# A chunked selective scan block on one core: the first step's sum kept in PSUM, its clip read from there, and first transposes a tile later

## The reference

```python
xr, gate = jnp.split(x @ W_in.T, 2, axis=-1)
xr = xr + t_emb[:, None, :]
xc = silu(depthwise_causal_conv4(xr, W_conv) + b_conv)
xn = (xc - mean(xc)) / jnp.sqrt(var(xc) + 1e-05) * ln_g + ln_b
Bm, Cm, dt = jnp.split(xn @ W_xproj.T, 3, axis=-1)
dt = jnp.tanh(dt @ W_dt.T + b_dt) * 0.01
Ad = 1.0 + dt * (-jnp.tanh(A_log))
Bd = Bm * jnp.minimum(jnp.linalg.norm(xn, axis=-1, keepdims=True), 1.0)
def step(h, inputs):
    ad, bd, xt, ct = inputs
    h = jnp.clip(h * ad[:, :, None] + bd[:, :, None] * xt[:, None, :], -10.0, 10.0)
    return (h, jnp.einsum('bd,bdh->bh', ct, h))
y = scan(step) + D * xn
out = x + y * silu(gate) @ W_out.T
```

## Time and profile before

| | |
|---|---|
| median of 3 runs | 2271.25 us |
| profiled execution | 2265.53 us, its span 2263.7 us |
| TensorE busy | 2018.2 us, 89% |
| GpSimd busy | 1805.1 us, 80% |
| VectorE busy | 1771.9 us, 78% |
| ScalarE busy | 1428.9 us, 63% |
| DMA, share of the 16 engines' time | 17.8% in the main queue |
| mean granted TensorE clock | 0.968 |

### The profile page before, as it was taken

How to read it: one execution, slowest core, us unless ns; L and a number is a source line. 1 busy time by engine, 2 the same in 40 slices (tenths; PEclk the granted TensorE clock), 3 DMA queues, 4 the chain that set the end, 5 groups by cost and what they waited for, 6 DMA issues and landing times.

```text
span 2263.7 us, 47166 instructions
## 1 busy us (share of the span) xinstructions
PE 2018.2 (89%) x16976; PEld 1486.0 (66%) x16976; DVE 1771.9 (78%) x2080; ACT 1428.9 (63%) x3462; POOL 1805.1 (80%) x1444
## 2 busy tenths in 40 slices
PE   5789989898989899889889899889899989899988
PEld 4567667666667666667666666666676666666655
DVE  3588788778787778887778887778887788887796
ACT  5667666666666666666666666666666666666643
POOL 1488888778888787888787888787888788888786
PEclk8799999999999999999999999999999999999999
DMA  4212111112111112111112111111111111121110
GB/s 164 57 48 59 46 51 46 50 48 60 46 49 40 55 51 60 46 49 41 55 51 60 43 52 41 55 51 55 45 55 41 54 52 49 50 56 41 46 51 15
DMA packets 81993, 118.09 MB, mean 52 GB/s; under 512 B 21840, under 2 KB 50896, under 8 KB 77088
## 3 DMA queue, kind: packets, MB, share of 16 engines
q1 hardware_dynamic: 81760, 115.07, 17.8%
HBM read 59.96 MB, written 9.18 MB: 31 GB/s over the span
## 4 chain that ended last, share of the span: by engine, by line
PE 69%; DVE 15%; issue 11%; ACT 4%; POOL 1%; SPq 1%; DMA 0%; DVEq 0%; POOLq 0%; ACTq 0%
PE ps_y L578 13%; DVE ks L978 9%; PE ps_job L447 8%; PE ps_job L452 8%; PE ps_job L493 7%; PE ps_fill L551 7%; PE ps_fill L542 7%; PE ps_y L558 4%; PE ps_job L465 4%; DVE h L934 3%; PE ps_job L459 2%; PE ps_job L474 2%; PE ps_y L564 2%; PE ps_job L487 1%; PE ps_job L483 1%
## 5 line engine op out<-in xcount | busy, mean ns | idle before, releaser
L1076 POOL TENSOR_TENSOR prod<-ks,crep 128x512 f32<-128x512 f32 x1024 | 1291.9, 1279 | 357.1 <-PE ps_y L578 268.1
L978 DVE TENSOR_TENSOR_SCAN ks<-low,ps_fill 128x512 f32<-128x512 f32 x1024 | 1221.3, 1206 | 385.9 <-PE ps_fill L551 383.0
L772 ACT COPY low<-ps_fill 128x512 f32<-128x512 f32 x1024 | 592.2, 582 | 546.7 <-PE ps_fill L542 542.4
L578 PE MATMUL ps_y<-c_sb,prod 128*128 128x128 f32 x4096 | 624.2, 275 | 2.7 <-POOL prod L1076 1.1
L578 PEld LDWEIGHTS ps_y<-c_sb,prod 128*128 128x128 f32 x4096 | 469.9, 142 | 124.1 <-issue 70.8
L542 PEld LDWEIGHTS ps_fill<-ts,xs 128*128 128x128 f16 x4096 | 315.9, 98 | 169.7 <-DVE ks L978 7.1
L542 PE MATMUL ps_fill<-ts,xs 128*128 128x128 f16 x4096 | 397.9, 220 | 5.4 <-DVE ks L978 4.4
L551 PE MATMUL ps_fill<-spans,pick 128*128 128x512 f16 x1024 | 390.5, 381 | 0.5 <-ACT low L772 0.3
L731 ACT ACTIVATE tap<-xr,cols_sb 128x128 f32<-128x128 f32 x768 | 251.5, 392 | 16.3 <-PE ps_job L465 16.2
L447 PE MATMUL ps_job<-x,w_in 128*128 128x128 f16 x3072 | 214.8, 221 | 20.4 <-POOL x L1046 7.8
L452 PE MATMUL ps_job<-w_in,x 128*128 128x512 f16 x768 | 209.4, 382 | 22.7 <-ACT xcT L742 22.7
(11 more groups left out here) (126 smaller groups left out, 2392.7 us busy)
## 6 DMA issues: line engine op xcount, KB each, us to landing
crep<-c_dram SPq DMA_DIRECT2D x32, 1024.0 KB, 4.8
xs<-xh SPq DMA_DIRECT2D x256, 64.0 KB, 2.0
xs<-xl SPq DMA_DIRECT2D x224, 64.0 KB, 2.0
xf<-in_xT SPq DMA_DIRECT2D x32, 256.0 KB, 2.8
res<-in_x SPq DMA_DIRECT2D x32, 256.0 KB, 2.6
out_dram<-res SPq DMA_DIRECT2D x32, 256.0 KB, 2.1
ts<-tth SPq DMA_DIRECT2D x128, 32.0 KB
ts<-tth SPq DMA_DIRECT2D x128, 31.0 KB
```

The lines of the kernel that those rows point to most:

```text
L578: last = mm(ps_y[:, cut], prod[:, s % HOLD, e, :], ident, start=False, stop=(u % 4 == 3 and q == 3 and e == QN - 1), is_transpose=True)
L772: copy(low[:, (TILES * k + s) % RING], ps_fill[:, (TILES * k + s) % RING]).then_inc(sem["low_copied"], 1)
L978: nc.vector.tensor_tensor_scan(ks[:, u % 2, QN * q:QN * (q + 1)].rearrange("d n t -> d (n t)"), low[:, g % RING], ps_fill[:, g % RING], 0. ...
L1076: tt(prod[:, i % HOLD], ks[:, u % 2, part], crep[:, p, part], ALU.mult).then_inc(sem["weighed"], 1)
```

## The change

1. The sum of the chunk's first step (L922 before) is written back into its PSUM bank instead of h1; one point later a clip per half (16 by 512) reads the bank and writes h1. The clip of the whole h1 at point 28 (L934) is gone. ScalarE's split at point 41 waits for the two halves.
2. z's first operation writes back into PSUM as well, and the second follows it directly at point 5 instead of 7.
3. The first flip of each half of y, with base and skip ahead of it, comes one tile later, just before the second flip.
4. In the table gate's first half goes from point 1 to 3, its second from 6 to 8, `nb` from 26 to 27, the carries from 30 and 35 to 32 and 36, with the points at which they are taken; GpSimd's root goes from tile 4 to tile 3.

```diff
-        JOBS = [(3, 2, "z", 0, 1, 1, 1), (1, 4, "gate", 0, 0, 2, 0), (6, 1, "hend", 0, -1, 2, 1),
-                (6, 4, "gate", 1, 0, 2, 0), (8, 1, "hend", 1, -1, 2, 1), (10, 1, "yT", 1, -1, 2, 1),
+        JOBS = [(3, 2, "z", 0, 1, 1, 1), (3, 4, "gate", 0, 0, 2, 0), (6, 1, "hend", 0, -1, 2, 1),
+                (8, 4, "gate", 1, 0, 2, 0), (8, 1, "hend", 1, -1, 2, 1), (10, 1, "yT", 1, -1, 2, 1),
...
@@ tensor: body(k, p) @@
                     t = s - LAG
-                    if t >= 0 and exists(k, 0):
-                        flip(k, p, t)
-                    elif t < 0 and exists(k, -1):
-                        flip(k - 1, 1 - p, t + TILES)
+                    if t % (4 * NQ) == 0:
+                        tiles = []
+                    elif t % (4 * NQ) == 1:
+                        tiles = [t - 1, t]
+                    else:
+                        tiles = [t]
+                    for t in tiles:
+                        if t >= 0 and exists(k, 0):
+                            flip(k, p, t)
+                        elif t < 0 and exists(k, -1):
+                            flip(k - 1, 1 - p, t + TILES)
@@ scalar @@
                 if point == 41 and exists(k, 1):
-                    act.wait_ge(sem["h1_done"], k + 2)
+                    act.wait_ge(sem["h0_taken"], 2 * (k + 2))
...
-                if point == 27 and exists(k, 1):
+                if point == 28 and exists(k, 1):
                     act.wait_ge(sem["nb16"], 2 * (k + 2))
@@ vector @@
                 if point == TAKE["z", 0] and exists(k, 1):
                     dve.wait_ge(sem["z_ready"], j + 1)
+                    stt(bank("z")[:, 0:3 * NS], sums[:, 0, :], tiny[:, 2:3], bank("z")[:, 0:3 * NS], ALU.mult, ALU.add
+                        ).then_inc(sem["z0"], 1)
                     since(dve, "zT_ready", j)
                     since(dve, "h0_ready", 2 * j)
-                    stt(z[:], sums[:, 0, :], tiny[:, 2:3], bank("z")[:, 0:3 * NS], ALU.mult, ALU.add
+                    dve.wait_ge(sem["z0"], j + 1)
+                    stt(z[:], bank("z")[:, 0:3 * NS], tiny[:, 1:2], sums[:, 1, :], ALU.mult, ALU.add
                         ).then_inc(sem["z_taken"], 1)
-                if point == 7 and exists(k, 1):
-                    dve.wait_ge(sem["z_taken"], j + 1)
-                    stt(z[:], z[:], tiny[:, 1:2], sums[:, 1, :], ALU.mult, ALU.add).then_inc(sem["z1"], 1)
...
-                    if point != TAKE["h0", i] or not exists(k, 1):
+                    if point != TAKE["h0", i] or not exists(k, 1) or first_chunk(j):
                         continue
 
                     half = slice(i * BANK, (i + 1) * BANK)
                     dve.wait_ge(sem["h0_ready"], 2 * j + i + 1)
+                    dve.wait_ge(sem["hend_taken"], 2 * k)
+                    dve.wait_ge(sem["decay0"], j + 1)
+                    stt(bank("h0", i)[0:NS], h1[:, half], first_decay[:], bank("h0", i)[0:NS], ALU.mult, ALU.add
+                        ).then_inc(sem["h0_sum"], 1)
+                for i in range(2):
+                    if point != TAKE["h0", i] + 1 or not exists(k, 1):
+                        continue
+
+                    half = slice(i * BANK, (i + 1) * BANK)
                     if first_chunk(j):
+                        dve.wait_ge(sem["h0_ready"], 2 * j + i + 1)
                         since(dve, "h1_high", j)
                         since(dve, "h1_low", j)
-                        nc.vector.tensor_copy(h1[:, half], bank("h0", i)[0:NS]).then_inc(sem["h0_taken"], 1)
                     else:
-                        dve.wait_ge(sem["hend_taken"], 2 * k)
-                        dve.wait_ge(sem["decay0"], j + 1)
-                        stt(h1[:, half], h1[:, half], first_decay[:], bank("h0", i)[0:NS], ALU.mult, ALU.add
-                            ).then_inc(sem["h0_taken"], 1)
+                        dve.wait_ge(sem["h0_sum"], 2 * (j - BATCH) + i + 1)
+                    tsc(h1[:, half], bank("h0", i)[0:NS], CLIP, -CLIP, ALU.min, ALU.max
+                        ).then_inc(sem["h0_taken"], 1)
...
-                if point == 28 and exists(k, 1):
-                    dve.wait_ge(sem["h0_taken"], 2 * (j + 1))
-                    tsc(h1[:], h1[:], CLIP, -CLIP, ALU.min, ALU.max).then_inc(sem["h1_done"], 1)
@@ gpsimd @@
-                    if s == 4 and exists(k, 1):
+                    if s == 3 and exists(k, 1):
                         pool.wait_ge(sem["squares"], j + 1)
                         tt(tiny[:, 5:6], tiny[:, 4:5], halfs[:, 1:2], ALU.pow).then_inc(sem["root"], 1)
```

More of the change, by code:

```diff
@@ L78 @@
 out_ready out_taken
-halo_saved conv_taken stats aggr rstd moments z1 zb ad scan_p recip weighted bound32 bound16 bound_all p_kept
+halo_saved conv_taken stats aggr rstd moments z0 zb ad scan_p recip weighted bound32 bound16 bound_all p_kept
 norm_in xa xg xn_done xh_done xl_done yT_high squares root nrm nb16 tt_done xd_done xd_used kend_done c_out c_in
-y_gated h1_done carry16
+y_gated h0_sum carry16
 h0_ready h0_taken h1_in0 h1_in1 decay0 h1_high h1_low
@@ L192, in since @@
             eng.wait_ge(sem[name], value)
-        JOBS = [(3, 2, "z", 0, 1, 1, 1), (1, 4, "gate", 0, 0, 2, 0), (6, 1, "hend", 0, -1, 2, 1),
-                (6, 4, "gate", 1, 0, 2, 0), (8, 1, "hend", 1, -1, 2, 1), (10, 1, "yT", 1, -1, 2, 1),
+        JOBS = [(3, 2, "z", 0, 1, 1, 1), (3, 4, "gate", 0, 0, 2, 0), (6, 1, "hend", 0, -1, 2, 1),
+                (8, 4, "gate", 1, 0, 2, 0), (8, 1, "hend", 1, -1, 2, 1), (10, 1, "yT", 1, -1, 2, 1),
                 (15, 1, "zT", 0, 1, 1, 1), (19, 4, "xr", 0, 2, 2, 0), (21, 1, "h0", 0, 1, 2, 1),
-                (24, 4, "xr", 1, 2, 2, 0), (24, 1, "h0", 1, 1, 2, 1), (26, 1, "nb", 0, 1, 1, 1),
-                (33, 11, "conv", 0, 2, 2, 0), (30, 1, "carry", 0, 1, 2, 1), (35, 1, "carry", 1, 1, 2, 1),
+                (24, 4, "xr", 1, 2, 2, 0), (24, 1, "h0", 1, 1, 2, 1), (27, 1, "nb", 0, 1, 1, 1),
+                (33, 11, "conv", 0, 2, 2, 0), (32, 1, "carry", 0, 1, 2, 1), (36, 1, "carry", 1, 1, 2, 1),
                 (40, 13, "out", 0, -1, 1, 1), (46, 9, "conv", 1, 2, 2, 0), (54, 1, "yT", 0, 0, 2, 1),
@@ L205, in build @@
         LAST = {(name, i): first + parts - 1 for first, parts, name, i, *_ in JOBS}
-        TAKE = {("z", 0): 5, ("gate", 0): 5, ("hend", 0): 6, ("hend", 1): 8, ("yT", 1): 10, ("gate", 1): 11,
-                ("zT", 0): 15, ("h0", 0): 21, ("h0", 1): 24, ("xr", 0): 23, ("nb", 0): 26,
-                ("xr", 1): 28, ("carry", 0): 30, ("carry", 1): 35, ("conv", 0): 44, ("out", 0): 53,
+        TAKE = {("z", 0): 5, ("gate", 0): 7, ("hend", 0): 6, ("hend", 1): 8, ("yT", 1): 10, ("gate", 1): 12,
+                ("zT", 0): 15, ("h0", 0): 21, ("h0", 1): 24, ("xr", 0): 23, ("nb", 0): 27,
+                ("xr", 1): 28, ("carry", 0): 32, ("carry", 1): 36, ("conv", 0): 44, ("out", 0): 53,
                 ("conv", 1): 55, ("yT", 0): 54, ("xt", 0): 58, ("xt", 1): 62}
@@ L671, in side @@
                     act.wait_ge(sem["nrm"], k + 2)
-                    act.wait_ge(sem["z1"], k + 2)
+                    act.wait_ge(sem["z_taken"], k + 2)
                     act_fn(z[:, 0:NS], z[:, 0:NS], ACT.Identity, scale=tiny[:, 6:7]).then_inc(sem["zb"], 1)
@@ L860, in side @@
                     dve.wait_ge(sem["aggr"], j2 + 1)
-                    since(dve, "z1", j2)
+                    since(dve, "z_taken", j2)
                     tsc(tiny[:, 0:1], mom[:, 1:2], EPS, None, ALU.add)
@@ L1018, in body @@
                         pool.wait_ge(sem["norm_in"], k + 3)
-                        since(pool, "z1", k + 2)
+                        since(pool, "z_taken", k + 2)
                         since(pool, "xa", k + 2)
```

## The result

The changed kernel takes 2132.1 us (median of 4 runs, 2129.3 to 2132.4) against 2271.2; the ratio is 0.9385, with an interval of 0.9368 to 0.9401. The forecast of 2088 was 44 us too low, and its range held the time. The profiled execution took 2132.4 us, its span 2130.6.

A forecast was written before the change was run, and what follows sets the result against it. TensorE's work plus its waits, mainly for a late VectorE, was taken as the bound. Terms sum to -5.9 us a step (68.27 to 62.4), 183 over 31 steps: 2088 us; own range 2045 to 2140, 8 of 10 within 2030 to 2180.

The forecast's parts named there:

- it is the SBUF to SBUF form that stands behind GpSimd: Step on VectorE's old clip L934: its 4.34 us come from the SBUF form waiting for GpSimd; PSUM halves take 0.68 each.
- A, second carry: TensorE's wait before the second carry matmuls L479: 0.1 of 2.1 us left, -2.0 a step, between 0 and -2.2.
- B, gate wait: TensorE's wait before L558 for VectorE's gate multiply: 1.2 of 2.4 us left, -1.2 a step, between 0 and -2.4.
- C, clock: Granted clock behind L558, fallen to 0.52 after two long waits, stays full: -1.7 us a step, or 0.
- D, stretch up to h0: GpSimd's root moves into its pause before tile 4, so h0 is released earlier: -0.9 us a step, between 0 and -0.9.
- E, start of the step: Gate's first part L452, moved behind z, waits 0.4 instead of 0.9 us for ScalarE's xcT: -0.5 a step.
- F, new wait: Gate 0 is taken behind ScalarE's L665, and gate 1 needs its bank: +0.4 us a step, from 0 to +1.2.
- The waits stay half: Rival, chance 0.14: TensorE's wait moves onto ScalarE's taps and copies, clock still falls; -3.0 a step, 2178 us.
- Halves behind GpSimd: Rival, chance 0.02: both clip halves still wait behind GpSimd, 2 x 4.34 us on VectorE, TensorE waits; 2405 us.
- no net gain: Rival, chance 0.03: the clip halves are cheap, but the schedule finds another wait of equal size; about 2268 us.

## Why the prediction was right and where it was wrong

**The clip: price right, reason wrong.** 0.68 was forecast for a half and 0.666 measured, 0.71 and 0.719 for the sums. But the step "it is the SBUF to SBUF form that stands behind GpSimd" failed as the account of the 4.3 us. The same form takes 0.66 us for the whole at point 26 and 3.31 for a half at point 28. The form has its share: at points 22 and 25 it waits 0.77 and 0.30 us in every steady step, where the one from PSUM never passed 0.679 in 64 instances. But the long wait needs the place. From one line with a median of 4.34 and a minimum of 0.92 I concluded on the form; the rows allowed the place just as well, and I did not list it. The Trainium skill (SBUF — State Buffer, section Who interferes with whom) has the shared ports go to whichever engine comes first, for a whole instruction, while the other is blocked. The products at 3.01 instead of 2.49 us agree. The clip that lets two borders of instructions go by does not agree; there the measurement decides. The same skill's VectorE: DVE Perf Modes, section on the TRN2 errata, gave an estimated 0.59 us for the whole clip in SBUF, where 0.656 was measured, and 0.66 for a half from PSUM against 0.666: PSUM does cost VectorE twice as much, and at VectorE's 50.8 of 63.7 us that is free.

The terms can be measured as TensorE's waits, tail counted, in one steady step: 1155.21 to 1223.46 before, 1157.29 to 1221.00 now. TensorE's work is the same, so the waits and the clock make up the whole difference of 4.5 us; what the table leaves out changed by less than 0.1.

| Term | Forecast | Measured | From, to |
|---|---|---|---|
| A, second carry | -2.0 | -1.9 | 2.27, 0.38 |
| B, gate wait | -1.2 | -1.6 | 2.43, 0.12 before L558 and 0.75 before the conv part |
| C, clock | -1.7 | -1.6 | pairs behind L558 3.41, 1.82 |
| D, stretch up to h0 | -0.9 | -0.05 | 0.93, 0.88 |
| E, start of the step | -0.5 | -0.6 | 0.92 before L452, 0.35 before a widen |
| F, new wait | +0.4 | +0.5 | 0, 0.51 |
| not in the sum: first carry | 0 | +0.7 | 0, 0.69 |

**Term B:** the wait shrank more than forecast and moved. Out's first part, at point 40, holds no matmul, only the wait for the bank of the second carry, and it stands ahead of the conv part of point 41 in TensorE's row. ScalarE's copies and VectorE's L970 behind them free that bank late: L970 ends at 1219.23, and TensorE goes on at 1219.3. The run with the copies ahead of the taps takes this away. The 1.5 us that the later transposes were to cover are the 1.44 a step of the run without them.

**Term C:** the size is right. That the fall needs more than one long wait is not borne out. In the run without the later transposes, of 30 waits of 2.2 to 2.7 us before L558, each with only 0.2 us before the second carry instead of 2.1, 7 were followed by the low clock; with both waits it was 28 steps of 32. So the second wait makes the fall regular, and a single long wait is not safe. Nor does show what the prediction took from it, since its row is the idle stretch itself; the 3.3 us behind that stretch are at 1.00 too in the trace.

**What failed** are two things in the sum. *The first is term D.* The stretch from the end of tile 0's transposes to h0, which GpSimd paces, did go from 9.63 to 8.70 us. But yT (0.44) and a tile (0.44) of TensorE's work now stand ahead of those transposes, so this stretch holds 0.88 us less work, and TensorE waits in it as long as before. The prediction saw 0.44 of this and still booked the full -0.9. The root's new place is worth 0.92 a step, as the run that undoes it shows; what it gained, the later start of the transposes in that stretch used up.

*The second is the sum's silence on one moved group.* In term A stood "nb from 26 to 27", but not that ScalarE's products L762 move with it from 27 to 28, behind the copy of low and xr's take. Their late end makes the first carry wait 0.69 us. Put back alone, L762 returned 0.34 a step and passed the rest on.

Together the two are 1.5 us a step, against 0.4 that term B gave beyond its forecast; the small rests of the others bring it to the missing 1.3. That the step of 62.4 is what TensorE reaches (62.5) once the carry's path on ScalarE is short is chance, since that kernel pays for term D too.

Outside the steady steps 8 us are missing as well: 31 steps of 4.55 would be 141 us, and the profiled executions lie 133 apart. The first L558 comes 4.6 us later than before (109.8 against 105.2), and the steps at both ends of the run gain less than those between. The 44 us hide most of this, because 5.7 us were added for the median and did not return: the changed kernel's median is its profiled time.

The inner range of 2045 to 2140 held the result, but it is not what the bounds of A to F give. Those add up to -7.7 and +0.7 us a step, 2032 to 2293.

**The rivals.** "The waits stay half" (2178) came nearest in kind: TensorE's wait did move onto ScalarE's taps and copies, 1.1 us of it, but without the clock's loss. "Halves behind GpSimd" did not come, and "no net gain" neither.

**Left open:** what, at point 28, keeps the waiting clip out at borders of GpSimd's instructions, when it gets in at the next one at points 22 and 25. Its length and tth are ruled out as the only reason. How long after a border it starts (0.46 us at 1106.58, some 0.01 at point 26) was not varied at one place, and a clip from PSUM at point 28 was not run.

## What to carry to other kernels

An instruction whose minimum is far below its median may be waiting, not working: before rewriting its form, move it by a point or two, which costs one number and here brought the full gain of the rewrite. Where a table of points is shifted, follow every instruction that hangs on each entry on every engine, not the named job alone; the one left out here was worth 0.34 us a step, some 11 us, when it was put back. Work moved out of a stretch that another engine paces turns into waiting there: count it against what the shorter stretch gains. When several changes remove the same stall, try each alone: 142 and 95 us made 139 together, and here one part alone did as well as all.

## What the runs showed of the hardware

- VectorE's clip 16x512 took 0.41 us in SBUF and 0.67 from PSUM, 16x1024 in SBUF 0.66, when nothing stopped it.
- At point 28 it waited 2.9 to 3.7 us in SBUF beside gapless work of GpSimd, past up to three borders of its instructions, and ended 0.3 to 0.6 us after GpSimd ran dry; at points 22 and 25 it waited 0.8 us at most in the steady steps, and at point 26, where it came just at a border, it made GpSimd wait 0.5. From PSUM it never took more than 0.68 at points 22 and 25.
- A wait of TensorE of 2.25 us before L558, with another of 2.1 ahead of it and 3.3 us of work between, was followed by a granted clock near 0.52 in 28 steps of 32. Where no second long wait stood ahead, 23 of 30 waits of 2.2 to 2.7 us before L558 left it at 1.00, and 7 were followed by 0.50 to 0.70 over the next 3.4 us.
